# Split products that alternate between two PSUM banks, in a cross-attention, self-attention and expert block

## The reference

```python
x = x + xattn(layernorm(x), ctx, Wq, Wkv, Wo)      # 16 heads of 32; 257 keys per sequence
x = x + attn(layernorm(x), wq, w_down, wk_up, wv_up, wo)  # rotary, latent keys and values
x = x + ffn(layernorm(x), Wr, W1, W2, W3)          # 8 experts, top 2, hidden 768

# xattn: Q = x Wq^T; K, V = ctx Wkv^T; softmax(Q K^T / sqrt(32)) V, then Wo^T
# ffn:   w, idx = top_k(x Wr, 2); softmax(w); sum over the chosen experts of
#        w * (silu(x W1[e]) * (x W3[e])) W2[e]
```

## Time and profile before

| | |
|---|---|
| median of 3 runs | 1495.09 us (1493.82 to 1500.4) |
| profiled execution, span | 1492.9 us |
| TensorE matmuls busy | 1434.5 us, 96% of the span |
| TensorE weight loads busy | 1281.3 us |
| VectorE busy | 1088.6 us |
| ScalarE busy | 807.5 us |
| GpSimd busy | 543.6 us |
| mean granted TensorE clock | 0.990 |

### The profile page before, as it was taken

One profiled execution on the slowest core, in us unless ns is written; L12 is line 12 of the kernel. 1 busy time (PEld: TensorE's weight loads), 2 busy tenths in 40 slices (PEclk: granted clock), 3 DMA queues, 4 the chain that ended last, 5 costly groups with the idle time before them and its releaser, 6 DMA issues. The chain is left out here.

```text
span 1492.9 us, 39481 instructions
## 1 busy us (share of the span) xinstructions
PE 1434.5 (96%) x14944; PEld 1281.3 (86%) x14944; DVE 1088.6 (73%) x1945; ACT 807.5 (54%) x1525; POOL 543.6 (36%) x810
## 2 busy tenths in 40 slices
PE   7999999999999999998999998799999999999998
PEld 6888888988888888887778786698999999999997
DVE  3676777767777677776667686797887878787785
ACT  4666666666666666654434434345555545555452
POOL 1222222221222222224866876453333333333232
PEclk9999999999999999999999999899999999999999
DMA  6301101000001100100011014179877878787871
GB/s 239 125 28 31 30 22 29 29 22 29 22 28 28 29 28 23 30 9 1 31 38 38 32 38 155 57 220 314 281 263 247 286 253 267 262 279 238 292 256 44
DMA packets 130734, 174.11 MB, mean 117 GB/s; under 512 B 16953, under 2 KB 89337, under 8 KB 130626
## 3 DMA queue, kind: packets, MB, share of 16 engines
q1 hardware_dynamic: 120242, 145.56, 30.1%
q0 software_dynamic: 10384, 27.05, 5.0%
HBM read 157.18 MB, written 19.06 MB: 118 GB/s over the span
## 5 line engine op out<-in xcount | busy, mean ns | idle before, releaser
L2229 DVE TENSOR_TENSOR split<-raw,split 128x1024 fp32r<-128x1024 f32 x204 | 242.3, 1220 | 7.2 <-ACT split L2169 6.0
L52 PE MATMUL bank<-split_xT,split 128*128 128x256 f32 x768 | 216.5, 282 | 0.4 <-DVE split L2229 0.2
L54 PE MATMUL bank<-split_xT,split 128*128 128x256 f32 x768 | 215.4, 281 | 0.0
L53 PE MATMUL bank<-split_xT,split 128*128 128x256 f32 x768 | 215.4, 280 | 0.0
L2169 ACT CAST split<-raw 128x1024 fp32r<-128x1024 f32 x202 | 203.2, 1048 | 6.9 <-DMA raw<-in_L_ffn_W_dram 3.2
L596 ACT ACTIVATE Pr<-xa_s,nmax 128x257 f32<-128x257 f32 x256 | 118.7, 473 | 124.9 <-DVE nmax L696 124.8
L2189 ACT ACTIVATE sl<-bank 128x256 f32<-128x256 f32 x115 | 44.2, 384 | 240.8 <-PE bank L54 223.5
L52 PE MATMUL xa_s<-split,split 128*128 128x258 f32 x512 | 150.5, 294 | 1.9 <-DVE split L628 1.9
L52 PEld LDWEIGHTS bank<-split_xT,split 128*128 128x128 f32 x768 | 144.9, 189 | 7.0 <-issue 2.8
L53 PEld LDWEIGHTS bank<-split_xT,split 128*128 128x128 f32 x768 | 145.0, 189 | 3.1
L53 PE MATMUL xa_s<-split,split 128*128 128x258 f32 x512 | 145.6, 284 | 0.0
(11 more groups left out here) (317 smaller groups left out, 3915.1 us busy)
## 6 DMA issues: line engine op xcount, KB each, us to landing
raw<-in_L_ffn_W_dram SPq DMA_DIRECT2D x207, 512.0 KB
raw<-in_ctx_dram SPq DMA_DIRECT2D x64, 256.0 KB, 2.6
out_dram<-x_res SPq DMA_DIRECT2D x16, 256.0 KB
xs<-xn SPq DMA_DIRECT2D x16, 256.0 KB
x_res<-in_x_dram SPq DMA_DIRECT2D x1, 3584.0 KB, 18.7
VL<-v_last_rows SPq DMA_DIRECT2D x128, 2.0 KB, 1.5
raw_o<-in_L_xattn_Wo_dram SPq DMA_DIRECT2D x1, 1024.0 KB, 6.4
raw_q<-in_L_xattn_Wq_dram SPq DMA_DIRECT2D x1, 1024.0 KB, 9.5
```

What stands on the lines that cost most here:

```text
L52: pe.matmul(out, lh, rh, start=start, stop=False)
L53: pe.matmul(out, ll, rh, start=False, stop=False)
L54: return pe.matmul(out, lh, rl, start=False, stop=stop)
L2229: vW.done(dve.tensor_tensor(lo, raw, hi.bitcast(F32), ALU.subtract), f"p{c}{q}")
```

## The change

A new function `products` takes several split products and issues the three kinds of matmul in turn: high x high for each, then low x high for each, then high x low for each. Neighbouring matmuls then write to different banks. It is used at three places with two products each: the scores by pairs of row blocks (0, 1) and (2, 3), the gather's two halves, and the two row blocks of the down projection. The number of matmuls and what each multiplies stay the same. In the scores the two waits on `v_PT` ahead of block 2 and block 3 become one ahead of the second pair, with the larger value. The increments of `pe_S` come on the last matmul of each block as before; these are now the last two matmuls of the pair. Gather and down projection keep their waits and their single increment.

```diff
+def products(pe, groups, start, stop):
+
+    for out, (lh, _ll), (rh, _rl) in groups:
+        pe.matmul(out, lh, rh, start=start, stop=False)
+    for out, (_lh, ll), (rh, _rl) in groups:
+        pe.matmul(out, ll, rh, start=False, stop=False)
+    return [pe.matmul(out, lh, rl, start=False, stop=stop) for out, (lh, _ll), (_rh, rl) in groups]
@@ scores
-                    for m in range(NQ):
-                        if some and m >= 2:
-                            pe.wait_ge(v_PT, 2 * s + m - 3)
+                    for pair in range(2):
+                        both = (2 * pair, 2 * pair + 1)
+                        if some and pair == 1:
+                            pe.wait_ge(v_PT, 2 * s)
                         for k in range(KL):
-                            mm = product(pe, bank_s[:, m, 0:KW], (QK_hi[:, k, m * P:(m + 1) * P], QK_lo[:, k, m * P:(m + 1) * P]),
-                                         (zT_hi[:, k, :], zT_lo[:, k, :]), k == 0, k == KL - 1)
-                        mm.then_inc(pe_S, 1)
+                            mm = products(pe, [(bank_s[:, m, 0:KW], (QK_hi[:, k, m * P:(m + 1) * P], QK_lo[:, k, m * P:(m + 1) * P]),
+                                                (zT_hi[:, k, :], zT_lo[:, k, :])) for m in both], k == 0, k == KL - 1)
+                        for op in mm:
+                            op.then_inc(pe_S, 1)
@@ gather_z
-                    for k in range(KL):
-                        for c in range(CH):
-                            mm = product(pe, bank_u[:, k],
-                                         (zn_hi[:, c, k * P:(k + 1) * P], zn_lo[:, c, k * P:(k + 1) * P]),
-                                         (PT_hi[:, c, :], PT_lo[:, c, :]), c == 0, c == CH - 1)
+                    for c in range(CH):
+                        mm = products(pe, [(bank_u[:, k], (zn_hi[:, c, k * P:(k + 1) * P], zn_lo[:, c, k * P:(k + 1) * P]),
+                                            (PT_hi[:, c, :], PT_lo[:, c, :])) for k in range(KL)], c == 0, c == CH - 1)[-1]
@@ down
-                    for r in range(2):
-                        mm = product(pe, bank_y[r][:], (a_hi[:, j % 2, r * P:(r + 1) * P], a_lo[:, j % 2, r * P:(r + 1) * P]),
-                                     (hi2[c][:, b, :], lo2[c][:, b, :]), j == 0, j == NH - 1)
+                    mm = products(pe, [(bank_y[r][:], (a_hi[:, j % 2, r * P:(r + 1) * P], a_lo[:, j % 2, r * P:(r + 1) * P]),
+                                        (hi2[c][:, b, :], lo2[c][:, b, :])) for r in range(2)], j == 0, j == NH - 1)[-1]
```

## The result

The changed kernel takes 1519.53 us (median of 4 runs, 1518.31 to 1520.81), beside 1495.15 us for the kernel before (4 runs). The ratio is 1.0154 with a 95% interval of 1.0138 to 1.0170: slower by 24.4 us. The prediction was 1519.5.

What follows compares the result with a forecast made beforehand. TensorE was taken to bound both the cross-attention loop and the experts' stage. Span 1492.9 + 25.2 of wait = 1518.1 us; the median 2.2 above gives 1520, less half a microsecond 1519.5; range 1503 to 1526.

Steps and rivals of the forecast that it cites:

- Zero for the rate of the alternating products: Scores, gather, down projection: a bank change at each of 2880 matmuls leaves the interval unchanged, zero us.
- the estimate that I made beside the Trainium skill's interval: If the bank explained 120 and 233 ns against the skill's 110 and 216, alternation would gain 38 us.
- 0.28 us from L641's end to the pair's second matmul: Scores, second pair: after the merged wait, the second matmul starts 0.28 us behind the end of VectorE's L641.
- the two steps near the end: Cross-attention loop: steps where L641 is early, ending before m=2 in the last; counted as paying nothing.
- 25.2 us in the sum, nothing given back: Cross-attention loop: delays of the merged wait sum to 25.2 us; later work hangs on the scores, so all reaches the end.
- common steps: Scores: 44 steps of the loop, each delayed 0.40 us by the merged wait, 17.6 us together.
- the last steps of the tiles: Scores: 15 steps with the longer delay, 0.47 us each, 7.05 us together.
- the third step: Scores: one step where m=2 already waited before the change; delayed 0.60 us.
- The clock as a rival: Loop: the bubble lowers the granted clock; a tenth of its matmuls at half rate adds 63 us, about 1580; chance 0.02.
- Increments, merged wait instruction, gather and down projection at nothing: Later semaphore increments in scores, one wait instruction fewer per step, unchanged waits in gather and down projection: no effect.
- The Trainium skill's rule on rotating banks: Scores: rotating independent groups through banks speaks against pairing m=2 with m=3; bank 2 is free while bank 3 is read.
- Criteria: Expected: new wait in about 60 steps, scores 0.4 us longer, intervals and experts' stage unchanged, loop about 25 us longer.

Runs made afterwards that it cites:

- the third experiment: Changed kernel, but in the second pair of scores blocks the first halves are serial behind their old waits and only the second halves alternate: 1498.88 us, ratio 1.0020.
- the second experiment: Changed kernel, but the second pair of scores blocks is serial again, each block behind its old wait; 2112 matmuls still alternate: 1497.09 us, ratio 1.0001.
- the first experiment: Kernel before, serial products everywhere, only the merged wait: block m=2 of the scores waits for both VectorE parts: 1519.97 us, ratio 1.0163.

## Why the prediction was right

*Zero for the rate of the alternating products*: right. Streams at 0.12 and 0.233 us per matmul after as before, and 2112 alternating matmuls leave the time at a ratio of 1.0001. The rows at the existing changes of bank, three kinds, had said so. The excess over the columns' time at 2.4 GHz (120 against 107.5 ns, 233 against 213) isn't the bank's; what it is, no run here tells. With it falls the estimate that I made beside the Trainium skill's interval (TensorE: Matmul & The Clock Gate, section Back-to-back issue gap): alternation brings no matmul nearer to columns / 2.4 plus 2.5 ns. That section of the Trainium skill gives the formula for an isolated matmul, which the prediction didn't say, and for a stream in which each matmul loads its weights about 131 ns at 512 columns; the trace's 233 ns agree with neither figure.

*0.28 us from L641's end to the pair's second matmul*: right and measured in four kernels, 0.05 or 0.06 for the first matmul and 0.28 for the second. One step of the trace of before was enough for the price. What I didn't see in it is that the same 0.28 also sets a threshold, which the third experiment found. In the prediction it touched only the two steps near the end, which I had counted at nothing and where m=2 started 0.09 us behind L641's end: their scores streams are 0.08 and 0.09 us longer in the changed kernel.

*25.2 us in the sum, nothing given back*: the loop's last step starts 24.9 us later. Each term stands as it was put: the scores streams grew by 0.40 us in common steps, by 0.47 in the last steps of the tiles and by 0.60 in the third step. The wait alone costs 23.7 us by the medians, the change 24.4. A three times longer stall is paid in full too, so the argument that everything behind the scores is anchored to them holds beyond this size.

*The number to the tenth*: luck. Two steps of the profiled execution differ for a reason that isn't in the sum, the granted clock, and they nearly cancel. In the second step's scores the clock rose sooner than before, which saved 1.05 us. In the last step of the fifteenth tile it fell: TensorE waited 2.10 us for ScalarE's copy, and then two scores matmuls took 0.43 us where 0.24 is usual (granted clock 0.50 from 652 to 654 us).

```profile
650.41 1.36 PE L421 MATMUL xa_s<-ident,Pr 128*128 128x128 f32 x8 [2.10 <-ACT QK L560]
651.42 0.78 PE L60 MATMUL xa_s<-split,split 128*128 128x258 f32 x2
651.99 0.63 PE L62 MATMUL xa_s<-split,split 128*128 128x258 f32 x2
652.42 0.63 PE L63 MATMUL xa_s<-split,split 128*128 128x258 f32 x2
```

That step grew by 1.37 us instead of 0.47. The kernel before has the same wait of 2.10 us at the same place and kept a clock of 1.00 behind it. Besides, the median of the kernel before, from which the forecast starts, was 1495.09 in its first three runs and 1496.28 in 23 later ones.

*The clock as a rival*: it doesn't carry the loss. Between 60 and 645 us, with the new pause in every step, the granted clock is 1.00, and the intervals are 0.12 us. Short stretches at the lower level near the end of the loop stand in kernels without the pause too (the second experiment's from 675 to 680 us).

*Increments, merged wait instruction, gather and down projection at nothing*: the second experiment carries the first pair's increments, the gather and the down projection, and shows nothing within 2.2 us; the first experiment has the one wait instruction fewer, and its loss needs no other term.

*The Trainium skill's rule on rotating banks* (Perfetto Trace Analysis, section Optimizing Tensor Performance): the trace after agrees. When m=2 started, VectorE had been done with its bank for about 0.6 us, half of L650's 1.29, and TensorE stood for the last 0.35 of that because the partner's bank was still being read. The 0.30 us that the prediction names there is the time from m=2's old start to the end of L641, not the time for which bank 2 was free.

*Criteria*: the wait shows about 60 times (58 in the weight loads' list), scores streams are 0.4 us longer, the intervals are unchanged. The experts' stage didn't shrink: from its first hidden product to its last down product it takes 533.1 us before and 536.6 after, beside 531.2 and 535.7 in the two experiments that alternate nowhere and have only the wait moved.

## What to carry to other kernels

When work is regrouped, the group waits for the latest of its members' producers at the position of its first member: compare that moment with the producer's end, step by step, before asking what the regrouping gains. If TensorE is the bound and all later waits in the step hang on this work, the delay is paid in full, once per step. To test a claimed hazard (here: same bank), look for the places where the old order already avoids it; to split PSUM traffic, let a copy take whole banks in the order in which they are needed, and then look again at the waits behind it, since work that comes sooner can run into the next one.

## What the runs showed of the hardware that I had not expected

- A wait costs TensorE time even when the waiting matmul isn't late: the second matmul behind it starts no sooner than 0.28 us after the producer's end (307.67 and 316.46 above). The weight loads show how, as far as the trace goes. In the changed kernel the load for m=2 starts only at 316.75, beside its matmul at 316.76, where the loads otherwise start one matmul ahead. In the common step of the third experiment, where L655 ended at 316.18, the waiting block's load starts at 316.23, 0.05 later, the next load 0.11 after it, and the second matmul 0.12 after that, at 316.46: together 0.28.

```profile
316.05 0.31 PEld L63 LDWEIGHTS xa_s<-split,split 128*128 128x128 f32 x2
316.75 0.30 PEld L60 LDWEIGHTS xa_s<-split,split 128*128 128x128 f32 x2 [0.40 <-DVE split L650]
...
316.23 0.19 PEld L52 LDWEIGHTS xa_s<-split,split 128*128 128x128 f32 x1
316.34 0.19 PEld L53 LDWEIGHTS xa_s<-split,split 128*128 128x128 f32 x1
```

- The waits list of the matmul side held 3.0 us of a loss of 24.4, that of the weight loads 20.4. For ScalarE's copy it held 4.4 us (weight loads 12.1), and 8.1 us went when the wait was removed.
- An interval of 0.40 us (changed kernel, 60 to 645 us) or 1.13 us (wait ahead of m=1, 60 to 720 us) instead of 0.12, once in every step, left the granted clock at 1.00.
